# A bias folded into a matrix product, and DVE work placed in the waits for GpSimd's power, in an audio tower kernel

## What is computed

```python
fr = jnp.fft.rfft(xp, axis=-1)                       # 101 bins
feats = jnp.concatenate([jnp.abs(fr), jnp.angle(fr)], axis=-1)
h = gelu(feats @ w1 + b1) @ w2 + b2                  # 202 -> 808 -> 128, 4096 tokens in 16 sequences of 256
h = h + attention(layernorm(h))                      # 8 heads of 64, sparsemax, ... @ W_out + b_out
h = h + experts(layernorm(h))                        # 8 experts, each takes its 1024 best tokens
```

## Time and profile before

| | us |
|---|---|
| median of 3 runs (936.76 to 937.72) | 937.27 |
| the profiled execution | 943.18 |
| its span, first to last instruction | 941.4 |
| busy in it: PE | 682.3 (72%) |
| busy in it: DVE | 614.2 (65%) |
| busy in it: ACT | 456.1 (48%) |
| busy in it: POOL | 214.3 (23%) |

### The profile page before, as it was taken

The page is one execution under the profiler, slowest core; times in us unless marked ns, Lnnn a source line. Parts: engine busy times, 40 slices in busy tenths (PEclk is TensorE's granted clock), DMA queues, the critical chain, the costliest instruction groups (busy, mean ns, idle before and its releaser), DMA issues.

```text
span 941.4 us, 12887 instructions
## 1 busy us (share of the span) xinstructions
PE 682.3 (72%) x3940; PEld 449.2 (48%) x3940; DVE 614.2 (65%) x2230; ACT 456.1 (48%) x663; POOL 214.3 (23%) x216
## 2 busy tenths in 40 slices
PE   5566959768996988399999998762221897667880
PEld 3234445345564564166575665441110565445660
DVE  2897568777977867697979879855668553423110
ACT  3773648437765756277778677752000331221310
POOL 1111100001000001001010010001003668888876
PEclk9878979978997998799999998885555897788895
DMA  5200000000000000000000000005000133443433
GB/s 153 77 0 1 0 2 1 2 2 13 1 2 12 1 2 12 1 2 13 1 2 13 2 13 2 13 1 151 0 0 20 43 52 67 68 68 65 68 34 28
DMA packets 34858, 23.72 MB, mean 25 GB/s; under 512 B 8246, under 2 KB 31366, under 8 KB 34768
## 3 DMA queue, kind: packets, MB, share of 16 engines
q0 software_dynamic: 11264, 8.40, 6.6%
q1 hardware_dynamic: 23292, 14.28, 5.4%
q10 hardware_dynamic: 212, 0.08, 0.0%
HBM read 14.36 MB, written 8.39 MB: 24 GB/s over the span
## 4 chain that ended last, share of the span: by engine, by line
DVE 30%; PE 29%; issue 12%; ACT 7%; POOL 7%; another core or an unknown queue 5%; DVEq 5%; DMA 2%; ACTq 1%; POOLq 0%; SPq 0%
DVE back L1043 7%; DVE top L1046 5%; PE ps L930 5%; DVE top L1036 4%; POOL out_dram L513 4%; PE ps L740 3%; PE ps L758 3%; PE ps L916 3%; PE ps L785 3%; PE ps L834 2%; PE ps L808 2%; PE ps L818 2%; ACT back L543 2%; DVE front L1236 2%
## 5 line engine op out<-in xcount | busy, mean ns | idle before, releaser
L543 ACT ACTIVATE front<-ps 128x1024 f32<-128x1024 f32 x128 | 127.8, 1026 | 41.0 <-PE ps L785 18.6
L635 ACT ACTIVATE front<-front,minus_tau 128x256 f32<-128x256 f32 x256 | 108.8, 499 | 66.1 <-DVE minus_tau L1125 65.0
L543 ACT ACTIVATE back<-ps 128x1024 f32<-128x1024 f32 x72 | 73.8, 1025 | 90.8 <-issue 74.0
L818 PE MATMUL ps<-ident,front 128*128 128x128 f32 x512 | 77.1, 300 | 52.0 <-ACTq L637 24.2
L513 POOL DMA_INDIRECT out_dram<-back x64 | 103.0, 1609 | 29.7 <-issue 18.3
L449 POOL CROSS_LANE_REDUCE more_all<-more 128x3 int32<-128x3 f32 x32 | 14.7, 460 | 410.7 <-DVEq L1062 410.7
L1043 DVE MATCH_REPLACE8 back<-top,front 128x256 f32<-128x256 f32 x256 | 101.4, 415 | 0.0
L818 PEld LDWEIGHTS ps<-ident,front 128*128 128x128 f32 x512 | 65.3, 155 | 74.8 <-ACTq L637 40.0
L1036 DVE MAX8 top<-front 128x8 f32<-128x256 f32 x256 | 86.8, 413 | 19.7 <-ACT front L543 10.8
L543 ACT ACTIVATE back<-ps,back 128x1024 f32<-128x1024 f32 x32 | 35.4, 1114 | 125.3 <-PE ps L916 57.3
L1046 DVE MAX8 top<-back 128x8 f32<-128x256 f32 x256 | 86.8, 413 | 2.4
(11 more groups left out here) (167 smaller groups left out, 1023.7 us busy)
## 6 DMA issues: line engine op xcount, KB each, us to landing
back<-in_L_ffn_W_dram SPq DMA_DIRECT2D x16, 256.0 KB
front<-in_x_dram SPq DMA_DIRECT2D x4, 750.0 KB, 4.4
rows<-xn SPq DMA_DIRECT2D x8, 256.0 KB, 2.5
out_dram<-h SPq DMA_DIRECT2D x1, 2048.0 KB, 9.6
back<-rows,back POOLq DMA_INDIRECT x64
out_dram<-back POOLq DMA_INDIRECT x64
wqkv<-in_L_attn_W_qkv_dram SPq DMA_DIRECT2D x1, 768.0 KB, 6.0
back<-in_L_ffn_b_dram SPq DMA_DIRECT2D x8, 64.0 KB
```

Of the source, the lines that this page charges most:

```text
L543: a.activation(dst, ps[s][:, 0:cols], func, **kw).then_inc(sems[f"free{s}"], 1)
L635: a.activation(prob[n % 2][:, r, :], sc[n][:, r, :], ACT.Relu, bias=minus_tau[:, n // 2, n % 2 * 4 + r:n % 2 * 4 + r + 1])
L818: last = nc.tensor.transpose(o[:, a_ * 512 + jb * SEQ + it * P:a_ * 512 + jb * SEQ + (it + 1) * P], prob[n % 2][:, 2 * a_ + it, jb * P:(jb ...
```

## The change

- The bias `tok_b2` becomes row 41 of the rest of the second product: it is loaded into `w2t` on partitions 40 and 104 of the last piece (two DMAs), `hid_r` is set to 1.0 everywhere at the start (ACT writes only the 40 rows of each half), and the four last matmuls of `emb` take 41 rows. `b2b`, its DMA and the step `embeddings` are gone; `tok_w_in` counts 6 DMAs instead of 5.
- The first norm reads its tiles from `emb` instead of `h`. What was the sum behind it, `h` + `bob`, is now `emb` + `bob` into `h`, and is issued between the signal to POOL and the wait for its answer. The drain ahead of it is gone.
- In the second norm, at the same place, the first four of the eight MAX8 of search 2 are issued, with their wait for score 4 and a drain; `largest` 2 behind the norm does the other four, with the wait for score 5. The very last second norm has a drain there.

```diff
         def layernorm(v, c, tiles, to, between):
...
             v.tensor_scalar(var_eps[:, :], mv[:, :, 1], EPS, None, ALU.add).then_inc(sems["ve_ok"], 1)
+            between()
             v.wait_ge(sems["rstd_ok"], c.up("rstd_ok"))
...
-            sp.dma_start(b2b[:, :], tok_b2.partition_broadcast(P)).then_inc(sems["tok_w_in"], 16)
+            for _, r1 in HALVES:
+                sp.dma_start(w2t[r1:r1 + 1, MT, :], tok_b2.rearrange("(a d) -> a d", a=1))\
+                    .then_inc(sems["tok_w_in"], 16)
...
-                            last = mm(o[:, at:at + D], hid_r[r0:r1, j % 2 * P:(j % 2 + 1) * P],
-                                      w2t[r0:r1, MT, :], start=False, stop=(j % 2 == 1))
+                            last = mm(o[:, at:at + D], hid_r[r0:r1 + 1, j % 2 * P:(j % 2 + 1) * P],
+                                      w2t[r0:r1 + 1, MT, :], start=False, stop=(j % 2 == 1))
...
+            v.memset(hid_r[:, :], 1.0)
             v.drain().then_inc(sems["zero_ok"], 1)
...
-            def largest(d, jobs):
+            def largest(d, jobs, heads=(0, 1)):
 
-                for u in range(2):
+                for u in heads:
                     emptied(jobs[u])
                 v.sem_inc(sems["held"], 1)
                 v.drain()
-                for r in range(8):
+                for r in range(4 * heads[0], 4 * heads[-1] + 4):
                     v.max(top[:, r, 0:8], sc[2 * d + r // 4][:, r % 4, :])
...
+                begun = None
                 for step, n in mine:
                     if step == "largest":
-                        kind, u = ("next", 2 * n) if n < 2 else ("score", 2 * n)
-                        largest(n, [jobs[kind, u], jobs[kind, u + 1]])
+                        largest(n, pair(n), (1,) if n == begun else (0, 1))
...
                     elif step == "second norm":
-                        second_norm(t - 1)
-                    elif step == "embeddings":
-                        embeddings(jobs["emb", 1], t + 2)
+                        begun = 2
+                        second_norm(t - 1, lambda: largest(2, pair(2), (0,)))
                     elif step == "first norm":
-                        first_norm(t + 2)
+                        first_norm(jobs["emb", 1], t + 2)
...
-            def embeddings(job, t):
-                tiles = h[:, ds(t * 4, 4), :]
+            def first_norm(job, t):
+                tiles = emb[:, :].rearrange("p (j d) -> p j d", d=D)
                 emptied(job)
                 v.sem_inc(sems["held"], 1)
-                v.tensor_tensor(tiles, emb[:, :].rearrange("p (j d) -> p j d", d=D),
-                                b2b[:, :].unsqueeze(1).to_broadcast([P, 4, D]), ALU.add)
-
-            def first_norm(t):
-                tiles = h[:, ds(t * 4, 4), :]
-                layernorm(v, c, tiles, xn).then_inc(sems["xn_ok"], 1)
-                v.drain()
-                v.tensor_tensor(tiles, tiles, bob[:, :].unsqueeze(1).to_broadcast([P, 4, D]), ALU.add)
-
-            def second_norm(t):
+
+                def kept():
+                    v.tensor_tensor(h[:, ds(t * 4, 4), :], tiles, bob[:, :].unsqueeze(1).to_broadcast([P, 4, D]), ALU.add)
+
+                layernorm(v, c, tiles, xn, kept).then_inc(sems["xn_ok"], 1)
```

26 lines of the change are left out of this document (13 added, 13 removed).

## The result

| | before, same chip | after |
|---|---|---|
| median of 7 runs each, us | 938.65 (936.76 to 940.61) | 933.16 (931.08 to 934.68) |
| ratio, 95% interval | | 0.9940 (0.9924 to 0.9957) |
| profiled execution, us (span) | 943.18 (941.4) | 934.68 (932.8) |
| end of the rounds in the trace, us | 645.81 | 640.08 |

The kernel is faster, clearly (by the interval 4.0 to 7.1 us), but the saving of 5.5 us is 3.8 us short of the forecast, and 933.16 lies above the range of 925.9 to 932.4. The two profiled executions are 8.5 us apart; 2.9 of these lie behind the rounds, in routing and experts' work that the change does not touch.

The account below looks back on a forecast made before the run. DVE was taken to bound most of rounds 0 to 3 and the last rounds, PE the stretch between. Terms 0.40 + 6.66 + 1.17 + 1.04 = 9.27 us, from 937.27 to 928.0 us; range 925.9 to 932.4.

Parts of the forecast that it names:

- What bounds the kernel: DVE from 157.1 to 399.3 us and again from 542.9, PE between; DVE's savings count only in DVE's stretches.
- The add's 0.76 us: Dropping the add of the embeddings' bias ahead of each first norm's statistics brings `xn` 0.76 us earlier.
- the root held up (0.36): In each first norm the sum in the wait makes POOL's root 0.36 us late, bounds 0 and 0.52.
- the sum out of the way (0.78): With the sum with `bob` ahead of the wait, the residual starts 0.78 us sooner behind each first norm.
- Four maxima in the wait, 1.04 us: Each second norm: 1.31 us less afterwards, scale 0.27 late, net 1.04 us; bounds 0.8 and 1.2.
- Rival 2: Maxima's gain becomes waits for scores before search 3 in rounds 1, 2, 3, 7; saving 5.1, time 932.2 us; chance 0.13.
- The cap of round 6: Search 3 of round 6 must wait for ACT's scores, so only 1.17 of 1.18 + 1.04 us counts.
- "It just fits" in round 2: Before search 3 of round 2, DVE saves 1.82 of the 1.98 us to ACT's end, so no wait comes.
- "PE's full stretch keeps its length": PE's full stretch, 399.3 to 542.9 us, stays equally long and comes 7 us earlier.
- The start's 0.40 us: The first `xn`, at 85 us, comes 0.76 - 0.36 = 0.40 us earlier.
- No eighth refinement: Sign to watch in the profile after: an eighth refinement of a search would show the prediction wrong.
- rival 3: Changed last bits of `h` cause one more refinement on DVE's path, costing 10.4 us; time 938.4 us; chance 0.07.

Follow-up runs that it names:

- one_input: Changed kernel with the sum with `bob` back behind the first norm and three single-input statistics in the wait for POOL's root; 932.45 us, a single execution.
- the two first fills: Kernel before and changed kernel, each with unread matmuls put into PE's idle gaps, twice as long as the gaps; 1.0474 and 1.0338 of the kernel before.
- filled pairs: Kernel before and changed kernel, each with unread matmuls sized to PE's idle gaps, on two chips; 0.9985 and 0.9869, then 0.9981 and 0.9884 of the kernel before.
- first pair of plain traces: First profiled executions of the kernel before and the changed kernel, neither with added matmuls; 943.18 and 934.68 us.
- second pair: The same two unchanged programs profiled once more, kernel before and changed kernel; 943.53 and 934.94 us, one execution each.
- filled kernel before: Kernel before with unread matmuls sized to PE's idle gaps; 0.9985 of the kernel before, median 937.96 us; run again on another chip 0.9981, 936.29 us.
- idle_mm_after: Changed kernel with 5, 7, 5 and 13 unread matmuls in PE's idle gaps; 0.9869 of the kernel before, median 928.32 us.

## Why the prediction was right or wrong

- **What bounds the kernel**: right. DVE's two pieces moved by nearly what was taken from DVE, PE's piece by the add's 0.72 us and by the length of the group at its head.
- **The add's 0.76 us, the root held up (0.36), the sum out of the way (0.78)**: right. The root in round 1 ends at 287.83, 0.88 us after the sum's end, where the prediction had 0.86; its length was 1.38 to 1.49 for a forecast of 1.37, which makes the sum's own gain 0.31 to 0.4 instead of 0.42 us. That it is the sum which holds the root up is shown by `one_input` against after; that it is its second input is not.
- **Four maxima in the wait, 1.04 us**: right, 0.93 to 1.01. Rival 2, that this gain turns into waits in rounds 1, 2, 3 and 7, is not what happened, though the time fell near its 932.2: in rounds 1, 3 and 7 no such wait came (search 3 starts 0.46, 0.45 and 0.31 us after DVE fell idle, as before). Only round 2's did, and in round 2 it took 1.24 us (1.68 less the 0.44 that every search has).
- **The cap of round 6**: right. The fourth piece is 1.51 us shorter; 1.45 was the forecast.
- **"It just fits" in round 2**: the first step that failed. The margin was 1.98 - 1.82 = 0.16 us, and it took for granted that the 16 products keep their 7.41 us. They took 8.70 and 8.56, at a granted clock of 0.81 and 0.82 instead of 0.95. That is shown: it explains ACT's lateness to 0.01 us, and at full clock the wait is gone. The margin itself was also read too wide: the 0.2 us from ACT's end to the first maximum, which the prediction counts in round 6, are left out here, and with them 1.82 us would have been 0.04 too many. The wait cost 1.24 and 1.10 us in the two traces, where the sum had nothing.
- **"PE's full stretch keeps its length"**: the second step that failed, at its head alone. The piece took 140.9 us before and 141.2 and 139.7 after, where 0.76 less was forecast. Behind the group at its head it is 0.72 less in both traces; the group has no fixed length (7.32 and 5.77 us after, 6.24 and 6.27 before), because PE starts it at the lower clock behind a gap.
- **The start's 0.40 us**: not seen in either pair (the piece is 0.83 and 0.01 us longer), but it scatters between 165.1 and 168.8 us over the plain kernels, so that the term can't be seen at all.
- **No eighth refinement**: right, rival 3 did not come.
- **From the profile to the runs**: a weak step. The forecast of 933.9 us for the profiled execution stands beside 934.68, but that agreement is in part luck: the trace of before had 295.6 us behind the rounds, where the sixteen traces of other kernels but the two first fills had 289.9 to 293.9 (its own second trace 295.6 again; why both traces of this kernel have it, no run shows), and 6.80 us for the first eight products. It was a long execution of its kernel, 943.18 where the median was 938.65 and the longest of seven 940.61, and the saving is not the same between two long executions as between two medians.

In sum, 9.27 was about the right size of what DVE is relieved of: DVE's pieces in the filled pairs show it for 6.66 of it (6.91 and 7.22), the fourth piece for 1.45 (1.51), the part of PE's piece behind its head for 0.76 (0.72), and the times of the filled pairs (9.64 and 8.76 us) agree within their noise. What the sum lacked is the length of the same matmuls behind PE's gaps. In the first pair of plain traces 1.24 + 1.08 = 2.3 of the 3.54 us missing at the end of the rounds are located there, in round 2's wait and in the group at the head of PE's stretch. In the second pair these two are 1.10 and -0.50, and the second fall of the clock in the last round takes most of another 1.71. The start, 1.23 and 0.41 us, is not resolved; the matmuls at its beginning vary by 3.1 us. The 3.8 us that are missing between the medians of the runs are not those of any one pair of traces, so how they divide stays open, and so does whether the change makes the low stretches longer on average. For that there is little sign: in the ten plain traces the group at the head takes a mean of 6.59 us in the three with the add and 6.52 in the seven without it, the 16 products of round 2 take 7.69 and 7.97.

## What to carry to other kernels

A saving on one engine is only worth its size if the next engine's work can follow, and where a margin of some tenths of a us decides, the length of that other work has to be given its own range: take the longest and the shortest that the trace shows for the same instructions, not the one in this place. Where PE has gaps ahead of work that the time hangs on, count a term for each that can go either way (here 1 to 2 us), and hold the clock with spare matmuls before judging edits of 1 us; after an edit that brings an engine to its data sooner, look again at waits that gather two producers, since they may be worth splitting now.

## What the runs showed of the hardware beyond the forecast

- Behind a gap PE's granted clock is 0.50, and one program leaves that level at different points in different executions: 7.32 and 5.77 us for the same group of the changed kernel, 6.94 and 3.85 us for the first eight matmuls of the filled kernel before.
- A second fall in the last round is there in some executions of a program and not in others (the last piece takes 32.08 and 33.79 us in the two traces of after, 34.38 and 32.14 in those of the filled kernel before). Where it is there the piece is 1.7 to 2.3 us longer; the gaps just ahead of it are no more than 0.7 us, but one of 6 to 8 us stands further ahead.
- A 128x128 by 128x512 matmul in fp32 stands in the trace as two and takes some 0.87 us at 2.4 GHz when such matmuls follow each other (26 entries, 13 matmuls of the program, in 11.32 us in `idle_mm_after`).
- An add of two inputs of 0.69 us on DVE, begun 0.08 to 0.17 us ahead of POOL's root over 4 elements a row, lengthens the root from 1.01 (1.06 in the first norm) to 1.38 to 1.49 us; three statistics with a single input, which write little (0.67 us), don't lengthen it.
